# Routing masks by ScalarE, unnormalised routing weights with their reciprocal in the row, and earlier gathers and slots in a 64-expert layer

## The reference, cut to what matters

```
ctx = causal_ema(x, tau_ctx); wg = sigmoid([x, ctx] @ Wg.T + bg); gated = x * wg
traces_d = causal_ema(gated * mod_d, tau_d)            # d = 0..7
temporal = sum_d traces_d * softmax(blend)_d
gate = sigmoid(temporal @ Wtemp.T + btemp); soma = gelu(x @ Wsoma.T + bsoma)
out = (soma * gate) @ Wout.T
z = (out - mean) / sqrt(var + 1e-5) * gamma + beta     # layer norm over 256 channels

probs = softmax(z @ router.T); topk_w, topk_ids = top_k(probs, 8)
topk_w = topk_w / sum(topk_w)
pos = running count of the expert among the earlier (token, choice) pairs; valid = pos < 128
y_e = (silu(z_e @ w_gate) * (z_e @ w_up)) @ w_down     # the rows of expert e
x = x + sum over the token's valid experts of topk_w * y_e + shared expert(z)
```

## Time and profile before

| | |
|---|---|
| median of 3 runs | 1110.4 us (1106.49 to 1114.75) |
| time of the profiled execution | 1111.76 us |
| its span | 1110.0 us, 14852 instructions |
| busy: PE / DVE / ACT / POOL | 952.2 / 746.3 / 460.8 / 667.0 us |
| layer 0 | 0 to 520 us |
| conditioning stage | 520 to 808 us |
| hand-over to the experts | 808 to 872 us |
| experts | 872 to 1086 us |
| last addition | 1086 to 1110 us |

### The profile page before, as it was taken

How to read it: one execution, slowest core, us unless ns; L and a number is a source line. 1 busy time by engine, 2 the same in 40 slices (tenths; PEclk the granted TensorE clock), 3 DMA queues, 4 the chain that set the end, 5 groups by cost and what they waited for, 6 DMA issues and landing times.

```text
span 1110.0 us, 14852 instructions
## 1 busy us (share of the span) xinstructions
PE 952.2 (86%) x4544; PEld 663.8 (60%) x4544; DVE 746.3 (67%) x1522; ACT 460.8 (42%) x835; POOL 667.0 (60%) x498
## 2 busy tenths in 40 slices
PE   5969899999999999987369889888688999889960
PEld 2534699899998999863125454444453665556640
DVE  2658466666666676524778999999876777667620
ACT  0320444555445544443446675757322222223320
POOL 1113444555445554315999999999852577777870
PEclk9989999999999999998689999999878999999995
DMA  4879234444344442134213742343259699996557
GB/s 153 276 261 349 63 77 113 90 89 95 87 118 86 89 100 39 21 66 105 96 38 96 245 150 69 114 138 117 90 167 320 179 262 264 259 254 144 94 72 156
DMA packets 93142, 155.46 MB, mean 140 GB/s; under 512 B 15784, under 2 KB 73328, under 8 KB 89936
## 3 DMA queue, kind: packets, MB, share of 16 engines
q1 hardware_dynamic: 51280, 90.61, 25.0%
q0 software_dynamic: 25296, 40.52, 20.3%
q10 hardware_dynamic: 16496, 23.49, 6.3%
HBM read 119.56 MB, written 43.42 MB: 147 GB/s over the span
## 4 chain that ended last, share of the span: by engine, by line
POOL 12%; issue 11%; PE 9%; DMA 7%; DVE 6%; ACT 2%; DVEq 2%; POOLq 2%; ACTq 0%
DMA odd_rows<-ys,slots 5%; POOL wide L652 4%; POOL wide L660 3%; DVE wide L1295 3%; PE bank L1685 3%; POOL xg L745 2%; DMA out<-ys,slots 2%; POOL out L752 1%; PE bank L1923 1%; DMA xg<-z_rows,slots 1%; POOL odd_rows L752 1%; POOLq L640 1%; ACT zrow L969 1%; ACT wide L919 1%; PE bank L1752 1%
## 5 line engine op out<-in xcount | busy, mean ns | idle before, releaser
L652 POOL TENSOR_TENSOR wide<-wide 128x1024 f32<-128x1024 f32 x64 | 156.6, 2461 | 31.8 <-issue 31.8
L1295 DVE TENSOR_TENSOR_SCAN wide<-bank,wide 128x512 f32<-128x512 f32 x128 | 149.4, 1210 | 22.3 <-POOL wide L652 22.1
L895 ACT ACTIVATE h_raw<-bank,b 128x512 f32<-128x512 f32 x128 | 88.1, 689 | 168.7 <-PE bank L1658 166.3
L1232 DVE TENSOR_TENSOR h_lo<-h_raw,h_hi 128x512 fp32r<-128x512 f32 x128 | 87.3, 692 | 91.8 <-ACT h_hi L899 91.8
L1673 PE MATMUL bank<-w_hi,h_hi 128*128 128x256 f32 x512 | 144.4, 282 | 0.1
L1673 PE MATMUL bank<-w_lo,h_hi 128*128 128x256 f32 x512 | 142.2, 278 | 0.0
L1673 PE MATMUL bank<-w_hi,h_lo 128*128 128x256 f32 x512 | 142.1, 278 | 0.0
L623 POOL DMA_INDIRECT x_rows<-ob,put x64 | 110.3, 1723 | 28.3 <-issue 16.0
L660 POOL TENSOR_TENSOR wide<-wide 128x1024 f32<-128x1024 f32 x46 | 108.4, 2358 | 11.9 <-issue 8.1
L919 ACT ACTIVATE wide<-wide,blend 128x512 f32<-128x512 f32 x128 | 84.0, 715 | 62.1 <-POOL wide L652 58.5
L1658 PE MATMUL bank<-ex_hi,w_hi 128*128 128x512 f32 x256 | 99.7, 389 | 2.5 <-issue 2.5
(11 more groups left out here) (242 smaller groups left out, 2002.6 us busy)
## 6 DMA issues: line engine op xcount, KB each, us to landing
wide<-in_mwp SPq DMA_DIRECT2D x40, 512.0 KB, 4.3
wide<-m_rows SPq DMA_DIRECT2D x16, 1024.0 KB, 4.8
w1s<-in_fW SPq DMA_DIRECT2D x8, 1024.0 KB, 5.0
w2s<-in_fW SPq DMA_DIRECT2D x8, 1024.0 KB, 5.3
own<-in_mwp SPq DMA_DIRECT2D x15, 512.0 KB, 4.9
head<-in_mwp SPq DMA_DIRECT2D x9, 512.0 KB, 4.3
xT<-in_xT ACTq DMA_DIRECT2D x8, 512.0 KB, 4.5
xt<-in_x ACTq DMA_DIRECT2D x8, 512.0 KB, 6.8
```

Of the source, the lines that this page charges most:

```text
L652: G.tensor_tensor(drive[n % DRIVES], gb[d % 2], md[d // HD][:, d % HD, :].unsqueeze(1).to_broadcast([P, CT, S]), ALU.mult).then_inc(c_u, 1)
L895: A.activation(h1_raw[f % 4][:, :], bank[:, 2 + f % 4, :], ACT.Gelu_apprx_tanh, bias=b1_0[:, bass.ds(e, 1), f]).then_inc(b_h, 1)
L1232: V.tensor_tensor(h1_lo[:, f, :], h1_raw[f % 4][:, :], h1_hi[:, f, :].bitcast(F32), ALU.subtract).then_inc(b_lo, 1)
L1295: o = V.tensor_tensor_scan(dst[:, c, :], decay[:, d:d + 1].to_broadcast([P, S]), drive[(D * b + d) % DRIVES][:, c, :], 0.0, ALU.mult, ALU.add)
```

## The change

Seven edits, all in layer 1:

1. `moments`: variance + eps and minus the mean are made by ScalarE, behind `weighted(b, 7)`. GpSimd keeps the power and the product.
2. `chosen_out`: for the first seven sequences ScalarE makes the mask from the replaced logits (`Sign` with a bias, then `Relu` straight into `mask_all`), behind the exponentials. VectorE's comparison and its copy fall away. For the last sequence VectorE compares straight into `mask_all`.
3. `route_weights`: one instruction takes the place of mask times exponentials and writes into `zrow`. The sum's reciprocal goes into a 65th column. The second product falls away, and VectorE multiplies the two numbers of each row when the expert's rows have come.
4. Rows of `zrow` and `z_rows` are 324 numbers long (1296 bytes) where they were 320 (1280 bytes).
5. The last sequence's rows are stored by ScalarE's queue, not GpSimd's.
6. GpSimd gathers for eight experts, not six, ahead of its wait for `c_ost`.
7. The token lists of experts 8 to 11, 12 to 15 and 16 to 19 are made one expert sooner.

```diff
-ZW = H + E1
+ZW = H + E1 + 4
...
-            return 4 * k - 8 - (0 if k < 4 else 1 if k == 4 else 2)
+            return 4 * k - 9 - (0 if k < 4 else 1)
...
             def rstd_of(q):
-                pool.wait_ge(c_mv, level(q))
+                pool.wait_ge(c_mw, level(q))
                 pool.wait_ge(c_no, level(q - 1, TT))
-                G.tensor_scalar(veps1[:, :], mv1[:, :, 1], 4 * EPS, None, ALU.add)
-                G.tensor_scalar(shift1[:, :], mv1[:, :, 0], -1.0, None, ALU.mult)
-                pool.drain()
                 G.tensor_tensor(rstd1[:, :], veps1[:, :], mhalf[:, :], ALU.pow)
...
-            pool.wait_ge(c_zr, level(B - 1))
-            last_rows(slice(H, ZW))
             wait_moved(pool, z_last, 1, 16)
...
-            for e in range(ROWS):
+            for e in range(8):
                 e_gather(e)
             pool.wait_ge(c_ost, level(B - 1, 16))
-            ahead_to = ROWS
+            ahead_to = 8
...
+            def moments(q):
+                act.wait_ge(c_mv, level(q))
+                act.wait_ge(c_no, level(q - 1, TT))
+                A.activation(veps1[:, :], mv1[:, :, 1], ACT.Copy, bias=4 * EPS)
+                A.activation(shift1[:, :], mv1[:, :, 0], ACT.Copy, scale=-1.0).then_inc(c_mw, 1)
...
+            def chosen_out(q):
+                act.wait_ge(c_top, level(q))
+                A.activation(sign[:, :, :], rep[:, :, :], ACT.Sign, bias=far[:, :], scale=-1.0)
+                act.drain()
+                A.activation(chosen(q), sign[:, :, :], ACT.Relu).then_inc(c_ma, 1)
...
                     exponentials(b - 2)
+                    chosen_out(b - 2)
                 if on(b):
                     weighted(b, 6)
...
                     weighted(b, 7)
+                if on(b - 1):
+                    moments(b - 1)
...
                 exponentials(B - 1)
+                act.wait_ge(c_zr, level(B - 1))
+                last_rows(slice(H, ZW))
                 shared_out(B - 1)
...
+                dve.wait_ge(c_ma, level(min(q - 1, B - 2)))
                 for j in range(TT):
-                    V.match_replace(rep[:, j, :], top8[:, j, :], lgp[:, j, :], -3.0e38)
-                dve.drain()
-                V.tensor_tensor(mask[:, :, :], rep[:, :, :], lgp, ALU.not_equal).then_inc(c_top, 1)
-                dve.drain()
-                V.tensor_copy(mask_all[:, :, q * TT:(q + 1) * TT].rearrange("p e t -> p t e"), mask[:, :, :])
+                    o = V.match_replace(rep[:, j, :], top8[:, j, :], lgp[:, j, :], -3.0e38)
+                if q < B - 1:
+                    o.then_inc(c_top, 1)
+                else:
+                    dve.drain()
+                    V.tensor_tensor(chosen(q), rep[:, :, :], lgp, ALU.not_equal).then_inc(c_top, 1)
...
-                V.tensor_tensor(mask[:, :, :], mask[:, :, :], ex[:, :, :], ALU.mult)
+                V.scalar_tensor_tensor(zrow[:, :, H:H + E1], rep[:, :, :], -1.0e38, ex[:, :, :], ALU.is_lt, ALU.mult)
                 dve.drain()
-                V.tensor_reduce(wsum[:, :], mask[:, :, :], AX.X, ALU.add)
+                V.tensor_reduce(wsum[:, :], zrow[:, :, H:H + E1], AX.X, ALU.add)
                 dve.drain()
-                V.reciprocal(wsum[:, :], wsum[:, :])
-                dve.drain()
-                V.tensor_tensor(zrow[:, :, H:ZW], mask[:, :, :], wsum[:, :].unsqueeze(2).to_broadcast([P, TT, E1]),
-                                ALU.mult).then_inc(c_zr, 1)
+                V.reciprocal(zrow[:, :, H + E1], wsum[:, :]).then_inc(c_zr, 1)
...
-                V.tensor_copy(share[i][:, :], xg1[e % ROWS][:, H + e:H + e + 1])
+                V.tensor_tensor(share[i][:, :], xg1[e % ROWS][:, H + e:H + e + 1], xg1[e % ROWS][:, H + E1:H + E1 + 1], ALU.mult)
```

More of the change, by code:

```diff
@@ L222, in build @@
         neg = sb("neg", [P, TT, E1])
-        mask = sb("mask", [P, TT, E1])
+        sign = sb("sign", [P, TT, E1])
+        far = sb("far", [P, 1])
         ex = sb("ex", [P, TT, E1])
@@ L280, in prep_start, with chosen @@
         def prep_start(k):
-            return 4 * k - 8 - (0 if k < 4 else 1 if k == 4 else 2)
+            return 4 * k - 9 - (0 if k < 4 else 1)
+        def chosen(q):
+            return mask_all[:, :, q * TT:(q + 1) * TT].rearrange("p e t -> p t e")
         def z_bank(q):
@@ L339, in build @@
         c_mdl = [sem(f"c_mdl{n}", 16) for n in range(2)]
+        c_mw = sem("c_mw")
+        c_ma = sem("c_ma")
         c_pad, e_pad = sem("c_pad", 0), sem("e_pad", 0)
@@ L629, in b_scatter @@
                     b_put_rows(r, j)
-            def last_rows(part):
-                pool.dma_start(z_rows[(B - 1) * S:TOK, part].rearrange("(t p) c -> p t c", p=P), zrow[:, :, part]).then_inc(z_last, 16)
             def rstd_of(q):
-                pool.wait_ge(c_mv, level(q))
+                pool.wait_ge(c_mw, level(q))
                 pool.wait_ge(c_no, level(q - 1, TT))
-                G.tensor_scalar(veps1[:, :], mv1[:, :, 1], 4 * EPS, None, ALU.add)
-                G.tensor_scalar(shift1[:, :], mv1[:, :, 0], -1.0, None, ALU.mult)
-                pool.drain()
                 G.tensor_tensor(rstd1[:, :], veps1[:, :], mhalf[:, :], ALU.pow)
@@ L678, in step @@
                     rstd_of(b - 2)
-                if b == B + 1:
-                    pool.wait_ge(c_no, level(B - 1, TT))
-                    last_rows(slice(0, H))
                 if on(b - 1):
@@ L961, in gate_out, with last_rows @@
                 o.then_inc(c_gt, 1)
+            def moments(q):
[3 more added lines that the diff above has]
+                A.activation(shift1[:, :], mv1[:, :, 0], ACT.Copy, scale=-1.0).then_inc(c_mw, 1)
+            def last_rows(part):
+                act.dma_start(z_rows[(B - 1) * S:TOK, part].rearrange("(t p) c -> p t c", p=P), zrow[:, :, part]).then_inc(z_last, 16)
             def normalise(q):
@@ L997, in step @@
                     exponentials(B - 2)
+                    chosen_out(B - 2)
                     shared_b_out(B - 2)
@@ L1000, in step @@
                     shared_out(B - 2)
+                    moments(B - 1)
                     normalise(B - 1)
+                    act.wait_ge(c_no, level(B - 1, TT))
+                    last_rows(slice(0, H))
                     return
@@ L1505, in front_only @@
             def front_only():
+                V.memset(zrow[:, :, H + E1 + 1:ZW], 0.0)
+                V.memset(far[:, :], -1.0e38)
                 ctx_scan(0, alpha)
@@ L1536, in _ @@
             prep(1, 3)
+            prep(2, 0)
             xgT_out(1)
@@ L1543, in _ @@
                 hidden(e)
-                if e == 0:
-                    prep(2, 0)
                 if e + 2 < E1:
                     xgT_out(e + 2)
-                if 0 < e < 4:
-                    prep(2, e)
+                if e < 3:
+                    prep(2, e + 1)
                 for k in range(3, E1 // 4):
@@ L1957, in _ @@
                     down(e - 2)
-                if 0 < e < 4:
-                    prep(2, e - 1)
+                if e < 3:
+                    prep(2, e)
                 for k in range(3, E1 // 4):
```

## The result

The changed kernel takes 1103.38 us (median of 20 runs, 1094.13 to 1109.9) where the kernel before took 1111.77 us beside it (20 runs, 1106.49 to 1116.62). The ratio is 0.9924, 95% interval [0.9905, 0.9944]: 8.4 us or 0.76% less. In a later set, beside the best version, the same kernel came to 0.9918 [0.9904, 0.9932]. The profiled execution took 1106.57 us with a span of 1104.8 us, 5.2 us less than the span before. That difference is smaller than 8.4 us because two single executions are compared. Their stages differ by some microseconds each, those that no edit touches too: the first L643 starts between 573.8 and 581.0 us over the fourteen profiles of this study, without order.

The account below looks back on a forecast made before the run. GpSimd was taken to bound the kernel. The terms 5.6 + 0.8 + 1.0 - 1.0 = 6.4 us, from the 1110.4 us median, gave 1104.0 us; the likeliest case's own range was 1099 to 1108, the overall ends 1096 and 1111.

Parts of the forecast that it names:

- The step: Conditioning stage: 1.0 us gained per step over six full steps, less 0.4 us; 5.6 us, ends 3.5 and 9.
- The term of the moments: Conditioning step: mean and variance moved from GpSimd to ScalarE gain 0.45 us per step, ends 0.3 and 1.5.
- The masks and weights: Conditioning step: VectorE's removed copy and second product stop delaying GpSimd's drive pairs, gaining 0.38 and 0.15 us per step.
- The last full step: Sixth full conditioning step: GpSimd already waits 1.99 us for a drive's scaled input, so 0.38 us of gain is lost.
- The hand-over: Between conditioning and experts: VectorE's shorter mask and weights bring the first rows sooner; 0.8 us, ends 0.2 and 1.8.
- Gathers and slots: Start of the expert stage: earlier gathers and slots let GpSimd's scatters and ninth gather start sooner; 1.0 us, ends 0 and 2.
- the sign: Start of the expert stage: the first scatter starts some 2 us sooner against TensorE's first expert.
- Longer rows: Expert stage gathers: 1296-byte rows off the 256-byte grid take 4% more of 26 us DMA time, costing 1.0 us.
- The sign that was named for it: Expert stage, 882 to 1000 us: GpSimd's waits for landed scatters stay the same if right; more waits if rows slow gathers.
- The full return: Conditioning step: removed instructions come back in full, 2.1 us a step, 13.3 us in all, 1097 us; chance 0.20.
- The rows' rival: Expert stage: rows off the grid slow the gathers, costing 10.5 us for 1113.5 us, at the end 1124 us; chance 0.13.
- The gains that do not reach the end: Whole kernel: half the step's gain and none of the experts' comes through, 2.6 us, 1108 us; chance 0.17.

Follow-up runs that it names:

- the best version: Changed kernel with edits 5 and 7 undone and one more filler turn of TensorE in the hand-over, against the kernel before: 1100.11 us, 0.9892.
- the experiment without the add: Changed kernel with VectorE's addition of the fourth trace replaced by a 128x1 memset, all waits kept: 1095.57 us, 0.9872 of the kernel before.
- the version with GpSimd's queue: Changed kernel with edit 5 undone, the last sequence's rows stored by GpSimd's queue again: 1101.89 us, 0.9911 of the kernel before.
- the extra turn: Changed kernel with edit 5 undone and one more TensorE filler turn behind the second token list's last turn: 1101.78 us, 0.9917 of the kernel before.
- the experiment on rows: Kernel before with only the rows lengthened from 320 to 324 numbers, the new ones unused zeros: 1111.98 us, 1.0014.
- The parts alone: Three runs on the kernel before: edit 1, 1107.85 us, 0.9976; edits 2, 3 and 4, 1107.5 us, 0.9968; edits 6 and 7, 1110.78 us, 0.9997.

## Why the prediction was right where it was, and wrong where it was

The forecast of 1104.0 us met 1103.4 us, inside its own range. That the two lie so close is in part luck. The gain of 6.4 us stands against 8.4 us with an interval from 6.2 to 10.6, and the kernel before came to 1111.8 us in these runs, where the forecast was made from 1110.4 us. The term of the step was too small, and two other terms, 1.8 us together, did not come at all.

**The step (forecast 5.6 us, measured 6.8).** The mechanism was right: GpSimd gets back what it executed, and what it waited goes elsewhere. The row of the fourth add and the group of powers show it, and the experiment without the add closes it. Over all sequences the power's group is now

```profile
L641 POOL TENSOR_TENSOR rstd_b<-veps,mhalf x8: 1017/1994/2012, 576.3 to 821.6; 128x4 f32<-128x4 f32 x8
```

against 1.04 us in the earlier trace rows. Two are short, the first sequence's (1.05 us) and the last one's (1.02 us), where no add stands beside them. The term of the moments was put at 0.45 us from the end of the add's hold; it measured 0.59 us. A better way to work it out is 2.59 us (L638's start to L641's end) less 2.00 us: the hold is 0.98 us long for whoever stands there, and the rest of the removed work, 0.22 + 0.22 + 0.15 us, comes back. The masks and weights were put at 0.38 + 0.15 us and measured 0.55 us; both pairs are at 4.66 us. L1402 does not lie like L1381: it takes 1.45 us (0.40 us where GpSimd is idle), and the wait is VectorE's, not GpSimd's. The first five steps gave 6.1 us, where the forecast had 5.0 (1.5 us of them in the third, which took 37.55 us before), and the sixth gave 0.7 us in this execution.

**The last full step.** The wait for a drive's scaled input was foreseen to take back 0.4 us, and took about 0.5 us in this execution (38.93 to 38.25 us is 0.68 us, a plain step gives 1.14 us). What makes the wait I had not seen. GpSimd and TensorE in this execution, in order of time:

```profile
781.65 2.37 POOL L652 TENSOR_TENSOR wide<-wide 128x1024 f32<-128x1024 f32 x1 [2.22 <-issue]
```

```profile
772.38 6.19 PE L1704 MATMUL bank<-wide,wtemp 128*128 128x512 f32 x7 [2.17 <-POOL wide L660]
```

And TensorE in the second execution of the same kernel, which has no such wait and a last step of 35.99 us:

```profile
771.27 3.70 PE L1704 MATMUL bank<-wide,wtemp 128*128 128x512 f32 x8 [0.50 <-POOL wide L660]
```

The gate's product takes 6.2 us or more where TensorE had stood idle for 2.17 us and was granted 0.50 of its clock (1.2 GHz) from 772 to 776 us, and 3.70 us where it had stood for 0.50 us and was at 1.00 (2.4 GHz) from 771 to 775 us. The gate, and behind it the scaled input, follow. Two executions of one kernel differ in it, by 2.3 us in this step, and the kernel before had the long product in its profile too, 6.53 us after 2.48 us of idle time. So the term of 0.4 us can't be judged from two profiles, and a part of the spread between executions is this.

**The hand-over (forecast 0.8 us, measured 0.0).** This step of the prediction failed. It took TensorE's other work for what stands last before the first rows, and moved it by what VectorE saves. For the changed kernel, VectorE and then TensorE in order of time:

```profile
830.85 1.28 DVE L1380 TENSOR_TENSOR mask_all<-rep,bank 128x256 bf16<-128x256 f32 x1
```

```profile
843.03 0.16 PE L1829 MATMUL bank<-Rx,before 32*32 32x4 bf16 x1 [1.89 <-DVE Rx L1422]
...
846.63 1.02 PE L1643 MATMUL bank<-flip,ident 128*128 128x512 f32 x2
847.59 0.41 PE L1834 MATMUL bank<-Rx,sel 32*128 32x131 bf16 x4
849.19 0.41 PE L1934 MATMUL bank<-ident,xg 128*128 128x128 f32 x2 [1.19 <-issue]
850.54 2.90 PE L1942 MATMUL bank<-own,xgT 128*128 128x384 f32 x4 [0.94 <-issue]
```

And TensorE in the kernel before, up to the first rows at 859.08:

```profile
856.68 1.91 PE L1624 MATMUL bank<-flip,ident 128*128 128x512 f32 x2
858.53 0.62 PE L1815 MATMUL bank<-Rx,sel 32*128 32x131 bf16 x4
```

Two things went unseen. First, VectorE's saving is not there. The mask in one instruction takes 1.28 us, where the two before took 0.42 + 0.74 us. Even so the mask is done at 832.13 and TensorE takes it at 832.48, behind its own filler work, so a shorter one would not have helped either. TensorE's part of the second list (L1829, L1810 in the kernel before) starts 20.3 us after the eighth L643 in both kernels.

Second, what ends the wait for the first rows has changed. In the kernel before the first gather lands 5.0 us after its start, at 857.4, and TensorE comes to the rows 1.7 us later, from its own work, at a granted clock of 0.50 (1.2 GHz) from 856.6 to 859.1. In the changed kernel the same two filler turns and the list's product run at 1.00 (2.4 GHz) from 846.6 to 848.0 and end 1.2 us sooner against the eighth L643. That is no gain, for now TensorE stands idle until 849.19. The profile doesn't name what it waits for ("issue"); in the program these transposes wait for nothing but the landing of their gather. This trace has not recorded that landing, but six other versions in which TensorE stood idle before these rows have, and in each the rows start 0.09 us after it. One is the version with edits 2, 3 and 4. VectorE, TensorE, and GpSimd's first gather (by its line, within 846 to 847 us):

```profile
850.39 0.69 DVE L1398 TENSOR_TENSOR hsA<-hsA,bank 128x512 f32<-128x512 f32 x1
```

```profile
853.66 0.66 PE L1936 MATMUL bank<-ident,xg 128*128 128x128 f32 x2 [3.50 <-issue]
```

```profile
L751 POOL DMA_INDIRECT xg<-z_rows,slots x1: 1084/1084/1084, 846.5 to 846.5; - x1
...
DMA to landing us min/median/max: 7.1/7.1/7.1
```

The gather lands at 853.57 and the rows start at 853.66. The same lines exclude a rival. VectorE's last product of the shared expert ends close before the rows in the changed kernel (848.9), which looks like a cause; here it is done at 851.1, 2.6 us ahead of the rows, and in the version without the fourth add it ends 0.9 us after they have started.

From the eighth L643 to the first rows it is 26.4 us in both kernels (27.7 us in the changed kernel's second execution). In the version with GpSimd's queue it is 26.4 us too, with the same 1.20 us of idle time, though its first gather starts 3.2 us sooner against the eighth L643: that gather takes 6.6 us to land. From its start at 846 to 851 us the DMA engines are full (share 1.05), all of it SyncE's queue (`q1`) with its loads. That the gather's rows wait behind these loads fits this, and it would make the queue and the start of the gather matter little; no run moved the loads to test it. What the idle time costs is the clock: behind it the first gate and up takes 2.90 us at 0.50 of the clock, and with the extra turn in the idle time it takes 1.53 us at 1.00. In the version with edits 2, 3 and 4, behind 3.50 us of idle time, it takes 2.90 us too, and the first `ys` comes 15.4 us after the rows where it was 13.1 us. The prediction had named TensorE's clock in the hand-over as what it can't forecast.

**The stores.** In the list of DMA issues the last rows (KB, us to landing) took 10.4 and 10.0 us by ScalarE's queue:

```profile
z_rows<-zrow ACTq DMA_DIRECT2D x1, 512.0 KB, 10.4
...
z_rows<-zrow ACTq DMA_DIRECT2D x1, 136.0 KB, 10.0
```

and by GpSimd's queue in the kernel before:

```profile
z_rows<-zrow POOLq DMA_DIRECT2D x1, 512.0 KB, 7.6
...
z_rows<-zrow POOLq DMA_DIRECT2D x1, 128.0 KB, 6.5
```

The size is not the cause: in the version with GpSimd's queue the 136 KB landed in 6.9 us and the 512 KB in 8.6 us. I had costed the queue at the time of issue only. The later gather cost nothing at the first rows, for the one that started 3.2 us sooner landed no sooner (above).

**Gathers and slots (forecast 1.0 us, measured 0.0).** The wait that was removed really went, and another took its place. GpSimd, then TensorE, in order of time:

```profile
865.13 1.63 POOL L747 DMA_INDIRECT out<-ys,slots  x1 [5.45 <-ACT ys L1097]
867.95 1.57 POOL L747 DMA_INDIRECT odd_rows<-ys,slots  x1 [1.18 <-ACT ys L1097]
```

```profile
860.88 0.16 PE L1829 MATMUL bank<-Rx,before 32*32 32x4 bf16 x1 [0.73 <-DVE Rx L1422]
...
864.05 0.41 PE L1834 MATMUL bank<-Rx,sel 32*128 32x131 bf16 x4 [0.19 <-DVE sel L1434]
...
867.92 0.40 PE L1823 MATMUL bank<-tri,mstat 128*32 128x128 bf16 x4 [0.68 <-DVE mstat L1418]
```

This step failed too. I took the time of `ys` from the earlier trace rows as fixed, and foresaw the scatter at once behind it. But the lists made one expert sooner lie in front of the first experts on TensorE, which waits for VectorE's part of them, 1.6 us in these three. What that costs is read where the clock is the same, from TensorE's first rows to the end of ScalarE's first three `ys`: 13.1, 16.0 and 19.2 us in the kernel before, 13.7, 17.1 and 20.9 us with edits 6 and 7 alone. The changed kernel with GpSimd's queue and the extra turn shows the same pair: 13.7, 17.1 and 20.9 us with the early lists, 13.1, 16.0 and 19.1 us with the late ones. So the lists cost 0.6, 1.1 and 1.8 us. In the changed kernel the first `ys` takes 15.1 us; the other 1.4 us are its slow gate and up. From the first rows to the first scatter it is 15.9 us where it was 14.3 us, not the 2 us less that I had named as the sign.

The gathers alone gave little. In the changed kernel with GpSimd's queue and late lists the first scatter comes 13.9 us after the rows, 0.3 us sooner than before, and the fourth 26.7 us after them, as before. I looked at the moved turns as things that arrive earlier, not as work moved past an engine that has no slack there.

**Longer rows (forecast a cost of 1.0 us, measured +1.6 us, from -1.1 to +4.3).** The size can't be judged; the rival of 10 us and more is excluded. The sign that was named for it did not show: from 882 to 1000 us GpSimd waited 9.2 us for landed scatters before, 7.4 us with the longer rows alone, and 7.0 us in the changed kernel. The share's multiplication, now two inputs from SBUF, takes 0.16 us (0.15 us as a copy), so GpSimd's gathers and scatters did not hold it up, as L1414's row had said. For the steady step the rule of the Trainium skill, SBUF — State Buffer, Who interferes with whom, holds: a VectorE instruction with two inputs from SBUF contends with a GpSimd instruction that reads SBUF, and here they wait for each other whole, 0.98 us for the add of 1024 numbers.

**The rivals.** The full return (1097 us) fell with the power at 2.0 us. The rows' rival fell with the experiment on rows. The gains that do not reach the end were half true: those of the hand-over and of the gathers did not reach it, those of the steps did. The parts alone sum to -2.7 - 3.6 - 0.3 = -6.6 us against -8.4 us together (edit 5 was not run alone on the kernel before); the intervals of 1.6 us and more to either side of each cover that.

## What to carry to other kernels

When two engines take turns at a resource, removing an instruction that stood in the other's hold returns its body, not its recorded time; read the body from the sequence where the other engine is idle. At a hand-over between stages, list everything that the first instruction of the next stage waits for (the landing of its gather, the engine's own work before it), with the time at which each is ready, and take the waits from the program: an instruction of another engine that ends just before is no cause if nothing waits for it. The gain of one input is worth nothing while another is as late. Work that is moved earlier is moved in front of something, and the engine that has to do it must have slack there.

## What the runs showed of the hardware

- The hold between GpSimd and VectorE is exclusive both ways: a 128x4 power on GpSimd took 1.02 us alone and 2.00 us beside VectorE's 128x1024 add; the add took 2.97 us issued beside a drive and 1.32 us otherwise. GpSimd's gathers and scatters did not cause it: L1414 took 671 to 674 ns among them.
- ScalarE's `Sign` and `Relu` behind an exponential needed no table load (0.49 us and 1.34 us for 128x256, the second written as bf16 and transposed).
- The comparison of 128x256 numbers took 1.28 us written as bf16, transposed, into `mask_all`, and 0.42 us with the same inputs into contiguous fp32; a copy with one input into the same place took 0.74 us, so the place alone doesn't explain it. Type and stride were not tried apart.
- With the DMA engines full (share 1.03 to 1.06) a store of 512 KB landed in 9.7 to 10.4 us by ScalarE's queue in three profiles and in 7.6 to 8.9 us by GpSimd's in eleven; one of 128 or 136 KB in 9.2 to 10.0 us and in 5.7 to 7.1 us. The share was read in ten of them.
- A gather issued to full DMA engines took 6.6 us to land in one version, and one issued 2.4 us later against the eighth L643 took 3.1 us: they landed within 1.1 us of each other.
- TensorE's clock at the gate's product was 0.50 in one execution of a kernel and 1.00 in another; the product was 2.5 us longer in the first, behind 1.7 us more of idle time, and GpSimd waited 2.2 us for its drive.
